# Perceiver block, first cross attention: three products in column strips, keys turned later in the slot

## The reference

```
q     = rms_norm(linear(layernorm(x), q_w, q_b), norm_q_w)
k_img = rms_norm(linear(context, k_img_w, k_img_b), norm_k_img_w)   # 257 rows
v_img = linear(context, v_img_w, v_img_b)
img_x = softmax(q k_img^T / sqrt(16)) v_img                         # by head
x     = x + linear(img_x, o_w, o_b)
```

## Time and profile before

| | us |
|---|---|
| median of 3 runs | 3255.65 (3253.79 to 3255.94) |
| profiled execution, its own time | 3256.4 |
| profiled execution, span | 3254.6 |
| PE busy | 3212.0 (99%) |
| PE weight loads busy | 2542.5 (78%) |
| DVE busy | 2550.1 (78%) |
| ACT busy | 2194.5 (67%) |
| POOL busy | 2196.2 (67%) |

### The profile page before, as it was taken

One profiled execution on the slowest core, in us unless ns is written; L12 is line 12 of the kernel. 1 busy time (PEld: TensorE's weight loads), 2 busy tenths in 40 slices (PEclk: granted clock), 3 DMA queues, 4 the chain that ended last, 5 costly groups with the idle time before them and its releaser, 6 DMA issues.

```text
span 3254.6 us, 110304 instructions
## 1 busy us (share of the span) xinstructions
PE 3212.0 (99%) x36167; PEld 2542.5 (78%) x36176; DVE 2550.1 (78%) x7862; ACT 2194.5 (67%) x6623; POOL 2196.2 (67%) x4241
## 2 busy tenths in 40 slices
PE   9999999999999999999999999999998999999999
PEld 7888888888766786777777777777775678999998
DVE  6677777777788767888788888888887888787777
ACT  5777777777756656777777777777775545555554
POOL 4666666666666456777777777777775686666665
PEclk9999999999999999999999999999999999999999
DMA  3111111111212242111111111111115650000000
GB/s 102 56 56 54 53 55 56 56 56 56 74 45 69 75 128 58 47 47 46 45 46 48 46 48 46 47 44 47 44 43 147 173 154 14 14 13 13 13 13 14
DMA packets 275886, 183.73 MB, mean 56 GB/s; under 512 B 116797, under 2 KB 272661, under 8 KB 275749
## 3 DMA queue, kind: packets, MB, share of 16 engines
q1 hardware_dynamic: 271109, 177.36, 19.2%
q10 hardware_dynamic: 4640, 4.59, 0.5%
HBM read 141.41 MB, written 36.21 MB: 55 GB/s over the span
## 4 chain that ended last, share of the span: by engine, by line
PE 59%; DVE 1%; DMA 1%; issue 0%; ACT 0%; POOL 0%; SPq 0%; ACTq 0%; DVEq 0%; POOLq 0%
PE bank_e L3134 12%; PE c_ps_a L1134 7%; PE b_ps_a L1100 7%; PE bank_e L3160 6%; PE s_ps_a L1107 6%; PE out_ps_a L1160 3%; PE a_ps_a L1111 3%; PE c_ps_a L1111 2%; PE b_ps_a L1111 2%; PE out_ps_a L1144 2%; PE c_ps_a L1193 2%; PE m_ps_r L2538 2%; PE c_ps_a L1172 1%; PE out_ps_a L1232 1%; PE c_ps_a L1183 1%; PE m_ps_r L2576 1%
## 5 line engine op out<-in xcount | busy, mean ns | idle before, releaser
L1264 ACT ACTIVATE probs_a<-s_ps_a,neg_max_a 128x257 f32<-128x257 f32 x1024 | 474.4, 476 | 83.1 <-DVE neg_max_a L1384 78.5
L1318 POOL TENSOR_SCALAR probs_a<-probs_a,gated_a 128x256 f32<-128x256 f32 x1024 | 473.8, 483 | 26.5 <-POOL gated_a L1327 26.3
L1384 DVE TENSOR_REDUCE neg_max_a<-s_ps_a 128x1 f32<-128x257 f32 x1024 | 424.4, 414 | 0.0
L574 POOL TENSOR_SCALAR probs_i<-probs_i,inv_sum_i 128x256 f32<-128x256 f32 x510 | 243.4, 491 | 134.2 <-DVE inv_sum_i L738 129.8
L1383 DVE TENSOR_TENSOR self_s_a<-s_ps_a,mask_a 128x32 f32<-128x32 f32 x1024 | 186.1, 182 | 135.8 <-PE s_ps_a L1107 135.8
L553 ACT ACTIVATE probs_i<-s_ps_i,neg_max_i 128x257 f32<-128x257 f32 x512 | 236.3, 474 | 58.6 <-DVE neg_max_i L812 56.9
L392 PE MATMUL a_ps_i<-w_k_i,ctx_t_i 128*128 128x256 f32 x1024 | 252.4, 389 | 0.0
L1134 PE MATMUL c_ps_a<-w_v_a,ctx_t_a 128*32 128x256 f32 x4096 | 248.8, 383 | 0.0
L379 PE MATMUL c_ps_i<-w_v_i,ctx_t_i 128*128 128x256 f32 x1024 | 247.5, 379 | 0.0
L1100 PE MATMUL b_ps_a<-ctx_t_a,w_qk_a 128*128 128x256 f32 x1016 | 242.1, 381 | 0.0
L812 DVE TENSOR_REDUCE neg_max_i<-s_ps_i 128x1 f32<-128x257 f32 x512 | 181.5, 416 | 52.9 <-PE s_ps_i L460 52.4
(11 more groups left out here) (454 smaller groups left out, 9422.2 us busy)
## 6 DMA issues: line engine op xcount, KB each, us to landing
ctx_t_i<-in_ctx_t SPq DMA_DIRECT2D x128, 256.0 KB, 2.7
ctx_t_a<-in_ctx_t SPq DMA_DIRECT2D x128, 256.0 KB, 2.7
mask_a<-in_L_xattn_mask SPq DMA_DIRECT2D x512, 4.0 KB, 1.5
v_bd_a<-v_self_a SPq DMA_DIRECT2D x512, 8.0 KB, 1.8
x_tok_i<-in_x SPq DMA_DIRECT2D x32, 128.0 KB, 2.0
x_res_i<-in_x SPq DMA_DIRECT2D x32, 128.0 KB, 2.5
x_after<-y_tok_i SPq DMA_DIRECT2D x32, 128.0 KB, 1.9
x_tok_d<-x_after SPq DMA_DIRECT2D x32, 128.0 KB, 2.2
```

The lines of the kernel that those rows point to most:

```text
L574: pool.tensor_scalar(probs[:, i, 0:2 * P], probs[:, i, 0:2 * P], inv_sum[:, i:i + 1], 1.0, ALU.mult, ALU.mult).then_inc(probs_ready, 1)
L1264: act.activation(probs[:, t, :], s_ps[:, g, 0:K], ACT.Exp, bias=neg_max[:, t:t + 1], accum_out=row_sum[:, t:t + 1]).then_inc(exp_done, 1)
L1318: pool.tensor_scalar(probs[:, t, 0:2 * P], probs[:, t, 0:2 * P], gated[:, t:t + 1], 1.0, ALU.mult, ALU.mult).then_inc(probs_ready, 1)
L1384: dve.tensor_reduce(neg_max[:, 4 * f + g:4 * f + g + 1], s_ps[:, g, 0:K], AX.X, ALU.max, negate=True).then_inc(max_ready, 1)
```

## The change

Three products go to strips of 32 weight columns: keys, values, and the last key's product with its values. Each 128x128 matmul becomes four of 128x32. In TensorE's order the values of batch n + 1 come before the turning of its keys (they were behind it), and no longer have a part after the item with b = 3. ACT's copy of the turned keys moves behind the squares. GpSimd gets a wait for its own scaling of the slot before.

```diff
 def values(at):
-    for r, c in ((0, 0), (0, 1), (1, 0), (1, 1))[begin:end]:
-        last = pe.matmul(c_ps[:, r * D:r * D + D], ctx_t[at.b(1)][:, c, r * P:r * P + P], w_v[:, c, :], ...)
-    if end == 4:
-        last.then_inc(v_full, 1)
+    for r, c in ((0, 0), (0, 1), (1, 0), (1, 1)):
+        for g in range(4):
+            rows = r * P + 32 * g
+            last = pe.matmul(c_ps[32 * g:32 * g + 32, r * D:r * D + D], ctx_t[at.b(1)][:, c, rows:rows + 32], w_v[:, c, :], ...)
+    last.then_inc(v_full, 1)
 def project(at):
...
-    last = pe.matmul(a_ps[:, r * D:r * D + D], ctx_t[at.b(2)][:, c, r * P:r * P + P], w_k[:, c, :], ...)
+    for g in range(4):
+        rows = r * P + 32 * g
+        last = pe.matmul(a_ps[32 * g:32 * g + 32, r * D:r * D + D], ctx_t[at.b(2)][:, c, rows:rows + 32], w_k[:, c, :], ...)
     last.then_inc(k_full, 1)
     if at.live(1):
+        ge(pe, v_ready, at.count(0))
+        values(at)
         if at.live(-1):
             pe.wait_ge(turn_read[1], at.count(-1))
...
         last.then_inc(k_turned, 1)
-        ge(pe, v_ready, at.count(0))
-        values(at, 0, 3)
-        if at.b() != 3:
-            values(at, 3, 4)
 def attend(at):
...
-    if at.live(1) and at.b() == 3:
-        values(at, 3, 4)
...
     for f in range(2):
-        last = pe.matmul(item_ps[:, f * P:f * P + P], v_last[:, f * P:f * P + P], p_rows, ...)
+        for g in range(4):
+            own = f * P + 32 * g
+            last = pe.matmul(item_ps[32 * g:32 * g + 32, f * P:f * P + P], v_last[:, own:own + 32], p_rows, ...)
 # scalar, slot
-    if at.live(1):
-        act.wait_ge(k_turned, at.count(1))
-        act.activation(k_n[:, :, 0:2 * P], b_ps, ACT.Copy).then_inc(k_ready, 1)
     if at.live(2):
         act.wait_ge(k_raw_ready, at.count(2))
         ...squares
+    if at.live(1):
+        act.wait_ge(k_turned, at.count(1))
+        act.activation(k_n[:, :, 0:2 * P], b_ps, ACT.Copy).then_inc(k_ready, 1)
 # gpsimd, slot
     if at.live(2):
+        ge(pool, k_scaled, at.count(1, 2))
+        pool.sem_inc(pool_waited, 1)
         pool.wait_ge(k_ms_ready, at.count(2))
```

More of the change, by code:

```diff
@@ L376, in tensor, with values @@
     def tensor(pe, before, ahead):
-        def values(at, begin, end):
-            for r, c in ((0, 0), (0, 1), (1, 0), (1, 1))[begin:end]:
-                last = pe.matmul(c_ps[:, r * D:r * D + D], ctx_t[at.b(1)][:, c, r * P:r * P + P], w_v[:, c, :], start=c == 0, stop=c == 1)
-            if end == 4:
-                last.then_inc(v_full, 1)
+        def values(at):
+            for r, c in ((0, 0), (0, 1), (1, 0), (1, 1)):
+                for g in range(4):
+                    rows = r * P + 32 * g
+                    last = pe.matmul(c_ps[32 * g:32 * g + 32, r * D:r * D + D], ctx_t[at.b(1)][:, c, rows:rows + 32], w_v[:, c, :], start=c == 0, stop=c == 1)
+            last.then_inc(v_full, 1)
         def project(at):
@@ L391, in project @@
                     for c in range(2):
-                        last = pe.matmul(a_ps[:, r * D:r * D + D], ctx_t[at.b(2)][:, c, r * P:r * P + P], w_k[:, c, :], start=c == 0, stop=c == 1)
+                        for g in range(4):
+                            rows = r * P + 32 * g
+                            last = pe.matmul(a_ps[32 * g:32 * g + 32, r * D:r * D + D], ctx_t[at.b(2)][:, c, rows:rows + 32], w_k[:, c, :], start=c == 0, stop=c == 1)
                 last.then_inc(k_full, 1)
             if at.live(1):
+                ge(pe, v_ready, at.count(0))
+                values(at)
                 if at.live(-1):
@@ L478, in attend @@
                     for f in range(2):
-                        last = pe.matmul(item_ps[:, f * P:f * P + P], v_last[:, f * P:f * P + P], p_rows[:, :, :].rearrange("p b q -> p (b q)"),
-                                         start=False, stop=True, skip_group_check=True)
+                        for g in range(4):
+                            own = f * P + 32 * g
+                            last = pe.matmul(item_ps[32 * g:32 * g + 32, f * P:f * P + P], v_last[:, own:own + 32], p_rows[:, :, :].rearrange("p b q -> p (b q)"),
+                                             start=False, stop=True, skip_group_check=True)
                 last.then_inc(out_done, 1)
@@ L528, in slot @@
         def slot(at):
-            if at.live(1):
-                act.wait_ge(k_turned, at.count(1))
-                act.activation(k_n[:, :, 0:2 * P], b_ps[:, :].rearrange("p (f n) -> p f n", f=2), ACT.Copy).then_inc(k_ready, 1)
             if at.live(2):
@@ L535, in slot @@
                     act.activation(sq[:, r, :], k_raw[at.b(2) % 2][:, r, :], ACT.Square, accum_out=k_ss[:, r:r + 1]).then_inc(k_ss_ready, 1)
+            if at.live(1):
+                act.wait_ge(k_turned, at.count(1))
+                act.activation(k_n[:, :, 0:2 * P], b_ps[:, :].rearrange("p (f n) -> p f n", f=2), ACT.Copy).then_inc(k_ready, 1)
             if at.live(1):
```

## The result

The changed kernel takes 3275.21 us (median of 4 runs, 3273.0 to 3277.68), the kernel before, in the same session, 3255.8 us (4 runs, 3253.79 to 3257.19). The ratio is 1.0062, with a 95% interval of 1.005 to 1.0074: slower by 19.4 us. The forecast was 3272 us, slower.

The account below looks back on a forecast made before the run. TensorE was taken to bound the phase without slack. Four slots: 27.08 us with strips, plus 0.56 (b = 1) and 0.27 (b = 3) for ACT's copies, 27.91 against 27.39; times 32, +16.6 us: 3272 us, range 3250 to 3282.

Parts of the forecast that it names:

- the strips' gain: Keys, values, last key on TensorE: strips save 0.31 us in four slots, 10 us over 32 groups, if nothing is late.
- the sum of 6.34: TensorE's slot with b = 1 in the new order: 6.34 us if nothing on another engine is late.
- The row of copies: ACT's serial copies from the turned keys on: the weighing's second half waits until 6.67, b = 1 slot 6.90.
- The wait for b_ps: Turned probabilities wait for ACT's key copy to free b_ps: 0.18 us in b = 1, plus 0.05 for the load.
- this term: Query item moved in b = 3, p_rows ready at 6.53: costed at nothing, bound 0.3 us in 23 of 32 groups.
- the forecast 7.05: Slot with b = 3: ACT's last copy delays the weighing's second half, 7.05 us, 0.27 over 6.78.
- b = 0 and 2: Slots with the 0.64 us longer item, which covers the copies and the b_ps wait: 6.98 us, nothing added.
- A: Rival, faster: ACT's copies do not hold PE, b = 1 slot 6.34; 3246 us; chance 0.13.
- B: Rival, no change: ACT keeps up, only the b_ps wait stays; 3260 us, up to 3263; chance 0.14.
- C: Rival, slower still: forecast plus late p_rows and 0.03 us per product; up to 3282 us; chance 0.12.
- 6.78: TensorE's slot with b = 3 in the new order: 6.78 us if nothing on another engine is late.
- D: Rival: every strip product's weight loads stand exposed on TensorE; 3374 us; chance 0.01.

Follow-up runs that it names:

- e5: Changed kernel with ACT's key copy put back ahead of the squares, so the squares stand behind it; 3347.88 us, ratio 1.0283.
- e1: Kernel before with only keys and last key's product in strips; values full, order and ACT as before; 3251.76 us, ratio 0.9988.
- e7: e1 with GpSimd's product for the last probabilities moved behind its fourth scaling, ACT's exponentials waiting for it; 3251.36 us, ratio 0.9989.
- e2: Changed kernel with all three products back at full 128x128 weights, leaving only the new order; 3279.61 us, ratio 1.0073.
- e3: Changed kernel with ACT's copy of the values ahead of its copy of the turned keys; 3269.09 us, ratio 1.0044.
- e6: e3 with the second half of the turned probabilities put in c_ps instead of b_ps; 3260.53 us, ratio 1.0015.
- e4: e1 with the values in strips too: all three products in strips, old order; 3292.65 us, ratio 1.0117.

## Why the prediction was right, and where its sizes were off

**What bounds, and the size of the strips' gain.** In all eight kernels of the table the lengthening of four slots, times 32, gives the measured difference within 3 us, so the whole difference is made in this phase; and e5 bears out that TensorE has no slack in it, as what goes into ACT's row comes out at the slot. The strips' worth was put at 10 us when nothing is late. No run shows that much. e1 shows 4.3 us without the values in strips; its slot with b = 1 stands 0.12 us over the sum of 6.34; I had put 0.1 of that down to late scaled probabilities, and e7, which took that wait away, got 0.04 back. In the new order the changed kernel lies 4.1 us below e2, each against its own before: 0.05 us in b = 1 and in b = 2 and 0.10 in b = 3 are gained, and 0.08 in b = 0 are lost (7.01 against 6.93), where the keys follow the last key and had no passage to save.

**The row of copies, b = 1.** Forecast: key copy at 4.26, last copy done at 6.61, slot 6.90. Measured 4.26, 6.60, 6.90. e2 shows it without strips, e3 takes 0.49 us out of the row and the slot falls by 0.31, down to the next wait; e5 puts 0.83 us in and the slot grows by 0.78. One step inside is off without changing the sum: the first half of the weighing was forecast at 6.15 and starts at 6.25 (514.69), since its loads start 0.11 us after their copy (513.93 + 0.62), not 0.04.

**The wait for b_ps.** Forecast 0.18 us and 0.05 for the load. From the item to the scores the changed kernel takes 513.94 - 512.50 = 1.44 us in b = 1; without a wait it would be 0.22 + 0.44 + 0.44 + 0.09 = 1.19, so 0.25 are lost, of which scaled probabilities that come late would cost a part anyway: e6, without the wait for `b_ps`, is 0.14 us shorter in b = 1 than e3 (6.45 against 6.59).

**b = 3: the right size for the wrong wait, in most groups.** The working had ACT's copies end last here, for 0.27 us and a slot of 7.05, and p_rows, at 6.53 of it, in time for a product due at 6.61; the slot is 7.12. DVE and TensorE's loads in the changed kernel, slot from 522.32:

```profile
528.56 0.29 DVE L802 TENSOR_TENSOR p_rows_i<-p_last_t_i,const_i 128x128 f32<-128x128 f32 x1
```
```profile
528.97 0.41 PEld L480 LDWEIGHTS out_ps_i<-p_rows_i,v_last_i 128*32 128x32 f32 x16
```

p_rows ends at 528.85, 6.53 into the slot, as forecast, but the product's loads start only 0.12 us after it, and its first matmul stands at 6.68; the working had counted no step between the two. I had put the bound of this term at 0.3 us and taken nothing.

The term is not small. The trace of the changed kernel holds both cases, as from some 690 us on DVE has no instruction on weights left ahead of p_rows, which then ends 5.75 us into the slot. DVE, then TensorE, in such a slot with b = 3:

```profile
863.43 0.29 DVE L802 TENSOR_TENSOR p_rows_i<-p_last_t_i,const_i 128x128 f32<-128x128 f32 x1
```
```profile
857.97 1.91 PE L395 MATMUL a_ps_i<-w_k_i,ctx_t_i 128*32 128x256 f32 x32
...
864.60 0.62 PE L480 MATMUL out_ps_i<-p_rows_i,v_last_i 128*32 128x128 f32 x16
865.04 1.91 PE L395 MATMUL a_ps_i<-w_k_i,ctx_t_i 128*32 128x256 f32 x32
```

Slots with b = 3 between 100 and 880 us of each trace, us:

| kernel | p_rows ends at 5.75 (7 or 8 slots) | p_rows ends at 6.53 (21 slots) |
|---|---|---|
| changed | 7.06 | 7.12 |
| e3, row of copies shorter | 7.03 | 7.11 |
| e6, and no wait for `b_ps` | 6.91 | 7.12 |

With p_rows early, the slot is the forecast 7.05 and falls when ACT's copies come sooner: the forecast mechanism is there. With p_rows late, in three quarters of the groups, it is 7.12 whatever ACT does: the last key's product sets it alone. So in most groups b = 3 would have lost the forecast 0.27 us without the copies, too. That the two chains reach the slot's end within 0.07 us of each other, and the sum came out near, was luck. The wrong wait shows in e3, where I expected 7.0 for this slot from the shorter row of copies and got 7.11. For e6 I did count p_rows, but too early: 7.0 forecast, 7.12 measured. With the rest out of the way, in e6, p_rows and q_bd cost 0.32 us in b = 3 (7.12 against 6.80 in e1), and that is nearly all that separates e6 from e1, some 10 us.

**b = 0 and 2.** Forecast 6.98 each; measured 7.01 and 6.98. The 0.03 us in b = 0 sits between values and key transposes (505.02 - 503.15 = 1.87 us, against 1.84). The records say where it comes from: in b = 0 keys and values are 1.94 us long and not 1.91, as the last of four strips runs 0.03 us later than elsewhere. That is so in e3 and e6 too, and not in e1, nor behind the slots with early p_rows (1.91 at 865.04 above). So it goes with the wait for p_rows in the slot before; why the strips then stand further apart was not tested.

**Adding up.** +0.52 us in four slots was forecast, +0.62 came: 16.6 against 19.4 us. The difference is 0.07 in b = 3 and 0.03 in b = 0. The rivals: A is out by the result, and by e3 and e5, which move nothing but ACT's copies and squares; B is out because e3 alone recovers 6.4 us with the wait for `b_ps` in place; C, late p_rows on top of the forecast, is the one that took part: 0.07 us above the forecast, but by itself the whole 0.34 over 6.78 in most slots with b = 3. D: thirty-two strips stream in 1.72 us, so their loads are hidden. The sentence of the Trainium skill (TensorE: Matmul & The Clock Gate, Part 3, The mechanism), by which loads overlap only with matmuls of other row groups, does not hold for column strips here. The same section also lets a load into the background weight buffer go ahead of matmuls in flight, which the prediction left out and with which 1.72 us would agree.

## What to carry to other kernels

When work is moved past its cover, follow what reads its result, and write down the whole serial row of the reader's engine, by start-to-start steps: here five copies in a row, each cheap, decided in b = 1, on an engine idle a quarter of the time. Do it for every engine whose input has moved: in b = 3 a chain on DVE, to which nothing was costed, ended last. Group products by weight shape, because each passage between strips and full weights cost TensorE 0.10 to 0.15 us in e4; but four strips side by side were no faster than one full matmul (1.72 against 1.73 us for a product). And where one wait goes, name the next before counting the gain: e3, e6 and e7 each met one close behind. A sum that comes out right does not show that each of its waits is the last one: look for slots in which only one of two chains is late.

## What the runs showed of the hardware

Sixty-four instructions for a product in strips (32 loads, 32 matmuls) stream in 1.72 us, as long as sixteen for the full one (1.73). A load that waits does not begin at the recorded end of what it waits for, and the step is not one figure: 0.12 us after DVE's p_rows (528.85 to 528.97 in the changed kernel), 0.05 us after ACT's key copy (512.70 + 0.60 to 513.35) and after its last probability copy (515.04 to 515.09), but 0.11 us after its first probability copy (513.93 + 0.62 to 514.66). So it does not go by the engine alone; what sets it was not tested. ACT's copies of 512 columns are recorded at 0.60 us but start 0.48 to 0.49 us apart, so a row of n of them takes less than n recorded lengths.
